# Who scales the normalised features h in the last layer: VectorE in place of ScalarE, behind step 15 of a chunk

## The reference

```python
h = relu(adj @ x @ gcn_w + gcn_b)
mu = h.mean(-1, keepdims=True)
var = h.var(-1, keepdims=True)
h = (h - mu) * rsqrt(var + EPS) * ln_g + ln_b      # the change is in this line
# _mamba(h): xz = h @ w_in; xc, z = halves; u = silu(conv4(xc) + conv_b)
# dt = softplus(...), B, C from u @ w_xp; dA = exp(dt * A); dBu = dt * B * u
hst = dA_t * hst + dBu_t;  y_t = hst @ C_t         # scan over the 2048 nodes
out = (y + u * D_skip) * silu(z) @ w_out
x = layernorm(x + out)
```

## Time and profile before

| what | us |
|---|---|
| median of three runs | 919.58 |
| the three runs | 916.18, 919.58, 920.45 |
| time of the profiled execution | 916.66 |
| span in that execution | 914.9 |
| last layer, from the first `h_spread` to the end | 631 to 914.9 |

### The profile page before, as it was taken

The page is one execution under the profiler, slowest core; times in us unless marked ns, Lnnn a source line. Parts: engine busy times, 40 slices in busy tenths (PEclk is TensorE's granted clock), DMA queues, the critical chain, the costliest instruction groups (busy, mean ns, idle before and its releaser), DMA issues. The chain is left out here.

```text
span 914.9 us, 11877 instructions
## 1 busy us (share of the span) xinstructions
PE 813.2 (89%) x4180; PEld 518.4 (57%) x4180; DVE 683.5 (75%) x976; ACT 521.1 (57%) x845; POOL 233.6 (26%) x135
## 2 busy tenths in 40 slices
PE   6999997999999999999789989989969889777565
PEld 6755547888888888874345559974322232311212
DVE  2986879999999999607942337872288699699996
ACT  2654546777777777634520127532667677776661
POOL 4000000000000000000000020001498789788992
PEclk9999998999999999999999979999979889997775
DMA  8589886220221121039410000000333515516310
GB/s 284 186 309 338 343 293 270 93 93 0 92 92 33 59 92 46 1 131 422 185 27 1 0 2 1 1 1 23 91 87 82 126 46 141 126 36 153 81 47 12
DMA packets 38960, 101.67 MB, mean 111 GB/s; under 512 B 6113, under 2 KB 11114, under 8 KB 32386
## 3 DMA queue, kind: packets, MB, share of 16 engines
q1 hardware_dynamic: 38354, 100.83, 33.2%
q10 hardware_dynamic: 560, 0.27, 0.1%
HBM read 75.60 MB, written 18.14 MB: 102 GB/s over the span
## 5 line engine op out<-in xcount | busy, mean ns | idle before, releaser
L1874 PE MATMUL PS<-big 128*128 128x256 f32 x768 | 194.5, 385 | 3.7 <-ACT big L1704 3.6
L221 PE MATMUL PS<-ident,big 128*128 128x128 f32 x1123 | 159.5, 282 | 28.4 <-ACT big L669 7.7
L221 PEld LDWEIGHTS PS<-ident,big 128*128 128x128 f32 x1123 | 137.7, 146 | 53.7 <-issue 19.3
L470 POOL TENSOR_TENSOR big<-big 128x1024 f32<-128x1024 f32 x64 | 149.8, 2361 | 10.8 <-DVE big L1444 10.6
L1874 PEld LDWEIGHTS PS<-big 128*128 128x128 f32 x768 | 133.7, 191 | 22.1 <-ACT big L1704 7.4
L1704 ACT ACTIVATE big<-PS 128x512 f32<-128x512 f32 x192 | 105.0, 598 | 58.5 <-PE PS L221 57.6
L431 POOL MEMSET big<- 128x16 f32 x1 | 0.1, 130 | 520.4 <-PE PS L842 520.4
L1444 DVE TENSOR_TENSOR_SCAN big<-PS,stripes,big 128x512 f32<-128x512 f32 x96 | 117.0, 1264 | 12.1 <-ACT PS L741 9.7
L2073 DVE SCALAR_TENSOR_TENSOR big<-big,rz 128x2048 f32<-128x2048 f32 x48 | 112.7, 2350 | 0.9
L2051 DVE CUSTOM_DVE_ANT_0 big<-big 128x2048 f32<-128x2048 bf16 x48 | 109.7, 2289 | 0.1
L1694 ACT ACTIVATE big<-big,ymin 128x2048 f32<-128x2048 f32 x48 | 96.3, 2006 | 15.0 <-DVE ymin L2051 14.7
(11 more groups left out here) (214 smaller groups left out, 983.1 us busy)
## 6 DMA issues: line engine op xcount, KB each, us to landing
big<-in_adj SPq DMA_DIRECT2D x16, 2048.0 KB, 8.6
big<-at_dram SPq DMA_DIRECT2D x4, 4096.0 KB, 28.0
at_dram<-big SPq DMA_DIRECT2D x3, 4096.0 KB, 16.7
big<-b_dram SPq DMA_DIRECT2D x32, 256.0 KB, 4.4
big<-big SPq DMA_DIRECT2D x24, 256.0 KB, 3.9
big<-b_dram SPq DMA_DIRECT2D x36, 128.0 KB, 4.0
at_dram<-big SPq DMA_DIRECT2D x1, 3072.0 KB, 18.6
big<-e_dram SPq DMA_DIRECT2D x3, 1024.0 KB, 6.2
```

The source lines that it names most:

```text
L221: return nc.tensor.transpose(PS[:, bank, col:col + P], src, ident[:])
L470: nc.gpsimd.tensor_tensor(dbu[k % 3], du2[c % 2][:, 2 * (n % 2):2 * (n % 2) + 2, :], bb[group % 2][:, pair_of(k) % 2, :].unsqueeze(1).to_b ...
L1874: m = nc.tensor.matmul(PS[:, 4 + k // 3, 0:256], hw[:, jt, h, :], qt[v % 4][:, 256 * c:256 * c + 256], start=(h == 0 and jt == 0), stop=(h ...
```

## The change

For chunks 1, 2 and 3, ACT keeps Ln and Exp of the root, and drops the offset (five activations), the four scalings and the semaphore `h_off`. DVE gets four `tensor_scalar` instructions that read PSUM bank 1 and write `ag_tiles`, by the helper that chunk 0 uses already. They stand behind scan(2) at k = 1, behind scan(16) and the weighing of step 15 at k = 15, and behind scan(32) and the weighing of step 31 at k = 31, with a wait for `h_root` ahead of them. `h_ready` is then counted up by DVE.

```diff
             def h_norm(c):
 
                 inverse_root(h_var, c + 1, 4 * c, 4, h_log, h_root)
-                offset(dj, h_root, c + 1, 4 * c, h_off, c)
-                h_scale(c, 1)
...
                 if k == 0:
                     h_spread(1, 1)
+                elif k == 1:
+                    h_rescale(1, 1)
...
                 if c < NCH - 2 and n == 14:
                     h_spread(c + 2, 1)
+                elif c < NCH - 2 and n == 15:
+                    h_rescale(c + 2, 1)
```

More of the change, by code:

```diff
@@ L208, in gnn_program @@
         c_mm, hcd_ready, hcp_ready = sem("c_mm"), sem("hcd_ready"), sem("hcp_ready")
-        h_off, o_off = sem("h_off"), sem("o_off")
+        o_off = sem("o_off")
         h_var, h_log, h_root, o_var, o_log, o_root = (sem("h_var"), sem("h_log"), sem("h_root"), sem("o_var"), sem("o_log"),
@@ L671, in shift_and_scale @@
                 m.then_inc(done, 1)
-            def h_scale(c, bank):
-                act.wait_ge(h_off, 2 * c)
-                shift_and_scale(ag_tiles, PS[:, bank, :].rearrange("p (s f) -> p s f", f=P), 4 * c, 4, dj, h_ready)
             def h_norm(c):
                 inverse_root(h_var, c + 1, 4 * c, 4, h_log, h_root)
-                offset(dj, h_root, c + 1, 4 * c, h_off, c)
-                h_scale(c, 1)
             def o_scale(c):
```

## The result

The changed kernel took 912.12 us in the median of six runs, beside 919.35 for six runs of the kernel before: a ratio of 0.9941, with a 95% interval of 0.9914 to 0.9968. (The quotient of the first two medians would be 0.9921; the runs of either kernel lie up to 6.5 us apart, and the interval holds both figures.) Either way it is faster, by an estimated 0.3 to 0.6%; the forecast was -3.0 us, 0.33%.

What follows compares the result with a forecast made beforehand. No engine bounds the whole layer; around steps 15 and 31 VectorE stalls 2.96 us for ScalarE's late decay. -1.7 - 1.7 + 0.4 = -3.0 us gave 913.7 or 916.6, set midway at 915.2 us, range 911.0 to 920.0.

Steps and rivals of the forecast that it cites:

- The stall at steps 15 and 31: VectorE's 2.96 us wait for ScalarE's decay inside scan(17) and scan(33); an earlier decay was to gain 1.7 us at each.
- a sign of being wrong: The prediction called itself wrong if, among other signs, the clock in the stretches had changed in the profile after.
- The VectorE page's figure: Skill page's estimate of 1.0 us for four rescalings from PSUM; the prediction used the profile row's 1.36 us instead.
- the full 1.7: Gain per place at steps 15 and 31, taken as kept whole though the convolution would start only 1.1 us earlier.
- rival a: Steps 15 and 31: TensorE hands the delay on, each place gives only 1.1 us, sum -1.8 us; chance 0.16.
- the bound of 1.1: Lower bound in us for the gain at one place, from the convolution's predicted earlier start; the upper was 1.9.
- The layer's start: Chunk 1's rescaling behind scan(2) ends later than ScalarE's scaling, so TensorE starts 0.4 us later: +0.4, bounds 0 and +0.6.
- ScalarE's wait for the convolution of chunk 1: At the layer's start, ScalarE's wait for TensorE's convolution, predicted to stay unchanged at 2.9 us.
- rival c: Layer's start: TensorE's longer stand keeps the clock low, +12.4 us, sum +9.4 us, 926.1 us; chance 0.07.
- rival d: Steps 15 and 31: VectorE waits for the root or the decay stays late; sum 0 to +3.1 us; chance 0.09.
- rival b: Layer's end: the clock rises from 1.2 GHz, another -3.6 us, together -6.6 us, 910.1 us; chance 0.13.
- The sum: -1.7 - 1.7 + 0.4 = -3.0 us over steps 15, 31 and the layer's start, bounds -3.8 and -1.6.

Runs made afterwards that it cites:

- e3: Changed kernel, but ScalarE still does all nine activations for chunks 2 and 3, results unread; 915.97 us, 0.9987 of before.
- e4: Changed kernel, but ScalarE still computes the five-activation offset of chunks 2 and 3, unread; 915.24 us, 0.9981 of before.
- e5: Kernel before, ScalarE still scaling, but making the next step's two decays ahead of the scalings at steps 15 and 31; 913.72 us, 0.9966.
- e10: Changed kernel with chunk 1 left to ScalarE, plus two unused matmuls behind each of steps 58 to 62; 909.95 us, 0.9933 of before.
- e9: Changed kernel plus 30 unused bf16 matmuls while TensorE waits for chunk 1's h; 911.18 us, 0.9956 of before.
- e7: Changed kernel plus two unused bf16 matmuls at the end of each of steps 58 to 62; 910.17 us, 0.9934 of before.
- e11: The changed kernel once more, unaltered, beside more runs of before; 913.47 us beside 916.25, 0.9967.
- e12: Changed kernel with chunk 1 left to ScalarE, 30 unused matmuls at the start and two behind each of steps 58 to 62; 909.64 us, 0.9927 of before.
- e6: Changed kernel plus 14 unused bf16 matmuls while TensorE waits for chunk 1's h; 913.44 us, 0.9972 of before.
- e1: Changed kernel with chunk 1 left to ScalarE, VectorE rescaling only chunks 2 and 3; 915.34 us, 0.9967 of before.

## Why the prediction was right, step by step

- **The stall at steps 15 and 31.** Right in mechanism and nearly in size. The decay was to start 3.72 us behind the table load; it did (731.00 - 727.28). VectorE's rescaling was to take 1.36 us; it took 1.36 and 1.36. The gain was put at 1.7 each with bounds of 1.1 and 1.9; it was 1.79 and 1.80. The clock, whose change the prediction named as a sign of being wrong, did change around step 15, from 0.72 to 1.00, but the length doesn't follow it. e3 and e4 show the shape that the working assumed, free while the stall lasts and paid when it is gone. e5 shows what it left unsaid, that moving the decays gets rid of the same stall.
- **The VectorE page's figure.** By the Trainium skill (VectorE: DVE Perf Modes, the section on the TRN2 errata) four rescalings would be an estimate of 1.0 us. They took 1.34 to 1.36 at all places; the page is too low for this form, and the row of before was right.
- **Whether the full 1.7 is kept (rival a).** The forecast took it so, since TensorE waits for VectorE within the next stretch. From the gating of chunk 0 to chunk 3's spread it is 53.85 us in both kernels. All of it is kept; rival (a) falls. The working on the convolution behind it was off, though. It was to start 1.1 us earlier; counted from the spread it started 10.32 us behind before and 7.75 after at step 15, 10.33 and 8.13 at step 31, so 2.6 and 2.2 us earlier, since TensorE's transposes moved up too (7.26 to 6.17 us behind the spread at step 15, and there at the higher clock: 0.63 us in place of 1.12). Nor did the bound of 1.1 hang on it: in e10, at the lower clock, the convolution of step 15 starts 9.24 us behind the spread, the 1.1 of the prediction, and the stretch behind it is 53.84 us all the same.
- **The layer's start.** +0.4 was predicted, with the reason that rescaling ends later than ScalarE's scaling did. TensorE started 0.33 us later in every kernel that has the change there, and e9 shows that its time there is on the path. But the term itself isn't seen in the result: in the trace of after the same stretch is 0.24 us shorter and not 0.4 longer, because the clock's level rose earlier in the skip product, and over all kernels the late scan is no later with the change than without it (25.53 and 25.60 us on average). Whether that is the change's doing or chance is open. Of the prediction's terms this is the one that the runs don't bear out, 0.4 of its 3.0 us. ScalarE's wait for the convolution of chunk 1, which was to stay at 2.9 us, was 2.63.
- **The clock turning at the start against us (rival c), nothing gained (rival d).** Neither happened: the level was back within the skip product or the sums behind it in all kernels. That the rise would move by the same 0.4 us as the start, as the prediction has it, isn't borne out: over the 8 us from the transposes' start the mean granted clock is 0.71 before and 0.79 after, which makes an estimate of 4.6 and 3.4 us at the lower level, so that, counted from scan(1), the rise came some 0.9 us earlier. And the rescaling waits for nothing (VectorE goes from 728.95 + 1.20 straight to 730.07).
- **The clock at the end (rival b).** The layer's end did come out 1.9 us shorter in the two profiles of after, of the 3.6 that the rival named. The size was too large, too: it is real as a price, but e7 and e10 make the same stretch 3 us shorter than before's at will. As an effect of this change it isn't shown.
- **The sum.** -3.0 forecast. From the cuts that belong to the change it is -1.79 - 1.80 = -3.6 us, or -1.79 - 1.80 + 0.33 = -3.3 us if the later start is counted in full; from the totals -3.0 (e11, 0.9967) and -5.4 (first comparison). The forecast time of 915.2 was set midway between two readings of a noisy median and lies 3.1 above the first measured one and 1.7 above the second; both lie in its range, the first 1.1 above its lower end. So the size of the two stalls was worked out, and that the sum comes so near is in part luck, since the totals can't tell -3.0 from -3.6. The chance of 0.29 for "faster by over 0.5%" was for this: the first ratio is past that line and the second is not.

## What to carry to other kernels

When an in-order engine is late for its partner, look first at what stands ahead of the late instruction in its queue, and by how much the work could be shortened before the partner's own work ends last; only that much is to be gained, here 1.8 of 2.6 us, and moving the awaited instruction up gains as much at that place as giving work away (in e5 0.5 us behind step 15 and up to 2.2 behind step 31 were lost again, in part by the clock). Work given to the engine that stands in the stall is free until the stall is gone. And where a gain is a third of a percent, cut the traces at the same instructions and compare lengths, since at the two steps they repeat to a hundredth of a microsecond where totals scatter by half a percent. Not every length does: look over several profiles which ones jump by themselves.

## What the runs showed of the hardware that I had not expected

TensorE's clock in a short burst of work behind a long stand is worth nearly as much as the change at one of the two steps: filling 8 us of standing with 30 small bf16 matmuls (about 0.22 us each, 6.64 us in e12) took 1.7 us off the late scan (e9), while 14 of them, with 5 us of standing behind them, left the lower level as it was (e6). And with no difference in the code, the stretch between chunk 0's spread and scan(1), all of it at the start of the layer, takes 33 or 35 us: 33 in before and e9, with a mean granted clock of 0.95 from 630 to 664 us, 35 in after and e1, with 0.90. e10, which is e1 but for the layer's end, has 33. What decides which it is stays open.
